# A convolutional LSTM in slots of a whole picture: each gate in two PSUM banks drained by one activation, gates in the order of need, waits counted per gate

## The reference

```python
def _s2s(hprev, w, b, wshift):
    hw = wshift(hprev)
    hd = _shift_down_h(hw)
    return jnp.einsum('bchw,oc->bohw', hd, w[:, :, 0]) + jnp.einsum('bchw,oc->bohw', hw, w[:, :, 1]) + b[None, :, None, None]
...
hmap = jnp.einsum('bchw,oc->bohw', x, w_i2s)
...
def step(carry, _):
    lc, lh, rc, rh = carry
    pre = jax.nn.sigmoid(_s2s(lh, w_left, b_left, _shift_right_w) + left_h)
    o, fg, ig, g = jnp.split(pre, 4, axis=1)
    lc = fg * lc + ig * g
    lh = o * jnp.tanh(lc)
    ...            # the same for rc, rh with the right weights
    return ((lc, lh, rc, rh), None)
(lc, lh, rc, rh), _ = jax.lax.scan(step, (zeros, zeros, zeros, zeros), None, length=h_)
rh = _shift_down_h(rh)
out_h = lh + rh
skip = jnp.einsum('bchw,oc->bohw', out_h, w_skip) + b_skip[None, :, None, None]
return x + skip
```

## Time and profile before

| | |
|---|---|
| median of 3 runs | 6539.12 us (6538.78 to 6540.97) |
| the profiled execution: own time, and span of its trace | 6541.35 us, 6539.6 us |
| busy in the span: PE, PEld, DVE, ACT, POOL | 94%, 56%, 93%, 69%, 39% |
| the untouched layers, from 1863 us on | 4677 us |
| the touched layer | 0 to 1863 us |
| in it the two loops over steps | about 14 to 899 and 935 to 1823 us |

### The profile page before, as it was taken

One profiled execution on the slowest core, in us unless ns is written; L12 is line 12 of the kernel. 1 busy time (PEld: TensorE's weight loads), 2 busy tenths in 40 slices (PEclk: granted clock), 3 DMA queues, 4 the chain that ended last, 5 costly groups with the idle time before them and its releaser, 6 DMA issues. The chain is left out here.

```text
span 6539.6 us, 155482 instructions
## 1 busy us (share of the span) xinstructions
PE 6169.2 (94%) x52289; PEld 3694.8 (56%) x52289; DVE 6112.0 (93%) x3734; ACT 4495.5 (69%) x9597; POOL 2554.8 (39%) x7010
## 2 busy tenths in 40 slices
PE   9999989999969999999999999999999999999996
PEld 2222226556536666666666666666666666666654
DVE  8888878888859999999999999999999999999995
ACT  7888868888836666666666666666666666666662
POOL 4555545555533333333333333333333333333321
PEclk9999999999979999999999999999999999999997
DMA  6666676666642121222212122121222212122114
GB/s 152 156 154 154 155 156 154 153 156 154 154 106 51 41 64 42 59 49 48 56 41 68 44 53 56 41 63 43 59 48 48 56 40 69 44 53 54 41 32 127
DMA packets 904175, 538.20 MB, mean 82 GB/s; under 512 B 695565, under 2 KB 813997, under 8 KB 903597
## 3 DMA queue, kind: packets, MB, share of 16 engines
q1 hardware_dynamic: 903597, 531.10, 34.8%
HBM read 142.32 MB, written 107.35 MB: 38 GB/s over the span
## 5 line engine op out<-in xcount | busy, mean ns | idle before, releaser
L1288 DVE TENSOR_TENSOR_SCAN states<-decay,enter_ps 128x1024 f32<-128x1024 f32 x2048 | 4471.9, 2262 | 55.2 <-PE enter_ps L848 42.4
L1039 ACT ACTIVATE decay<-rate_ps 128x512 f32<-128x512 f32 (+1 forms) x4096 | 2221.6, 594 | 342.9 <-PE rate_ps L834 147.6
L848 PEld LDWEIGHTS enter_ps<-s_steps,s_tokens 128*128 128x128 bf16 x16384 | 1602.8, 129 | 1358.2 <-DVE states L1288 1062.8
L848 PE MATMUL enter_ps<-s_steps,s_tokens 128*128 128x128 bf16 x16384 | 2142.0, 310 | 237.8 <-DVE states L1288 228.0
L834 PE MATMUL rate_ps<-s_wide,s_decays 128*128 128x256 bf16 x8192 | 1318.4, 283 | 8.7 <-DMA s_wide<-rates_dram 8.4
L266 POOL TENSOR_TENSOR entered<-gates 128x512 f32<-128x512 f32 x512 | 901.1, 1760 | 890.2 <-ACT gates L229 890.2
L1211 POOL TENSOR_TENSOR product<-decay,states 128x16 f32<-128x16 f32 x1920 | 465.5, 242 | 1789.2 <-ACT decay L1039 1785.6
L1046 ACT COPY enter_ps<-at_first 128x16 f32<-128x16 f32 x1920 | 337.5, 176 | 1189.1 <-PE enter_ps L848 1134.2
L878 PE MATMUL y_ps<-states,spread 128*32 128x512 f32 x8192 | 1090.3, 604 | 2.4 <-issue 2.4
L834 PEld LDWEIGHTS rate_ps<-s_wide,s_decays 128*128 128x128 bf16 x8192 | 903.1, 118 | 67.5 <-issue 9.9
L186 PE MATMUL pre<-rows,weights_left 128*32 128x512 f32 x8192 | 903.1, 595 | 26.7 <-DMA skip_b<-b_skip 13.7
(11 more groups left out here) (160 smaller groups left out, 2364.4 us busy)
## 6 DMA issues: line engine op xcount, KB each, us to landing
rows<-feat SPq DMA_DIRECT2D x1024, 132.0 KB, 2.4
rows<-feat SPq DMA_DIRECT2D x512, 128.0 KB, 2.4
s_steps<-steps_dram SPq DMA_DIRECT2D x4096, 8.0 KB
rows<-feat SPq DMA_DIRECT2D x512, 127.8 KB, 2.4
s_wide<-rates_dram SPq DMA_DIRECT2D x1024, 32.0 KB, 1.9
s_tokens<-tokens_dram SPq DMA_DIRECT2D x2048, 16.0 KB, 2.0
rates_dram<-parts SPq DMA_DIRECT2D x64, 384.0 KB, 3.3
steps_dram<-parts SPq DMA_DIRECT2D x64, 384.0 KB, 3.5
```

Of the source, the lines that this page charges most:

```text
L848: mm = pe.matmul(out.rearrange("p h l -> p l h"), tokens[s][:, k, :], steps[s][:, k, :, d:d + half], start=True, stop=True)
L1039: act.activation(decay[i][:, half, at:], rate_ps[h][:, :, at:], ACT.Exp).then_inc(decay_ready, 1)
L1288: dve.tensor_tensor_scan(out, factor, term, 0.0, ALU.mult, ALU.add).then_inc(scanned, 1)
```

## The change

A slot becomes one stream's whole picture: 4 slots a step, 256 in all. A gate takes two PSUM banks (`pre[g]`), which eight matmuls fill (a *fill*) and one sigmoid of 128x1024 drains. The fills come in the order input, candidate, forget, output (`FILLS`), and `pre_ready` and `gates_ready` count fills, so that POOL starts after two gates, `forget` after three, and PE refills a gate's banks as soon as that gate of the slot before is drained. ACT puts the tanh of slot k behind the first gate of slot k+1 and ahead of the three others. DVE does `new_features` of slot k ahead of `forget` of slot k+1. All operations of ACT, DVE and POOL work on 1024 elements in a partition, half as many of them. `gates` has two buffers instead of four, of twice the size.

```diff
-GATE_RING = 4
+GATE_RING = 2
+FILLS = (2, 3, 1, 0)
...
-        pre = [ctx.enter_context(nc.psum_tensor(f"pre{c}", [128, 4, BANK], F32)) for c in range(CHUNKS)]
+        pre = [ctx.enter_context(nc.psum_tensor(f"pre{g}", [128, CHUNKS, BANK], F32)) for g in range(4)]
...
-                        for c in range(CHUNKS):
-                            k = s * CHUNKS + c
-
-                            pe.wait_ge(gates_ready, START + (r * STEPS + t) * SLOTS + k - CHUNKS + 1)
-                            for g in range(4):
+                        for i, g in enumerate(FILLS):
+                            pe.wait_ge(gates_ready, START + ((r * STEPS + t) * SLOTS + s - 1) * 4 + i + 1)
+                            for c in range(CHUNKS):
                                 for q in range(GROUP):
-                                    mm = pe.matmul(pre[c][32 * q:32 * q + 32, g, :],
+                                    mm = pe.matmul(pre[g][32 * q:32 * q + 32, c, :],
...
+            def gate_value(r, t, k, i):
+                g = FILLS[i]
+                act.wait_ge(pre_ready, fill(r, t, k, i))
+                if i == 0:
+                    act.wait_ge(feat_ready, slot(r, t, k - GATE_RING))
+                act.activation(gates[k % GATE_RING][:, g, :], pre[g][:, :, :].rearrange("p c l -> p (c l)"), ACT.Sigmoid,
+                               bias=biases[side(k)][:, g:g + 1]).then_inc(gates_ready, 1)
...
                     if following:
-                        gate_values(r, t + (k + 1) // SLOTS, (k + 1) % SLOTS)
+                        gate_value(r, t + (k + 1) // SLOTS, (k + 1) % SLOTS, 0)
                     squash(r, t, k)
+                    if following:
+                        for i in range(1, 4):
+                            gate_value(r, t + (k + 1) // SLOTS, (k + 1) % SLOTS, i)
...
-                        pool.wait_ge(gates_ready, slot(r, t, k))
+                        pool.wait_ge(gates_ready, fill(r, t, k, 1))
...
-                    dve.wait_ge(gates_ready, slot(r, t, k))
+                    dve.wait_ge(gates_ready, fill(r, t, k, 2))
...
                     after = t + (k + 1) // SLOTS, (k + 1) % SLOTS
+                    new_features(t, k)
                     if following:
                         forget(*after)
-                    new_features(t, k)
-                    if following:
                         enter(*after)
```

More of the change, by code:

```diff
@@ L72, in conv_phase @@
         cell = [sb(f"cell{s}", [128, LEN]) for s in range(STREAMS)]
[L73 to L76, removed]
+        gates = [sb(f"gates{i}", [128, 4, LEN]) for i in range(GATE_RING)]
+        forgot = [sb(f"forgot{i}", [128, LEN]) for i in range(2)]
+        entered = [sb(f"entered{i}", [128, LEN]) for i in range(2)]
+        squashed = [sb(f"squashed{i}", [128, LEN]) for i in range(2)]
         weights = [sb("weights_left", [128, 128]), sb("weights_right", [128, 128])]
@@ L209, in slot, with fill @@
             return START + (r * STEPS + t) * SLOTS + k + 1
+        def fill(r, t, k, i):
+            return START + ((r * STEPS + t) * SLOTS + k) * 4 + i + 1
         def steps(eng, r, first, body):
@@ L222, in _ @@
             act.wait_ge(weights_in, START + 7 * DMA)
[L224 to L231, removed]
+            def gate_value(r, t, k, i):
[5 more added lines that the diff above has]
+                               bias=biases[side(k)][:, g:g + 1]).then_inc(gates_ready, 1)
             def squash(r, t, k):
-                c, s = k % CHUNKS, k // CHUNKS
                 act.wait_ge(cell_ready, slot(r, t, k))
-                act.activation(squashed[c][:, :], cell[s][:, BANK * c:BANK * c + BANK],
-                               ACT.Tanh).then_inc(squashed_ready, 1)
+                act.activation(squashed[k % 2][:, :], cell[k][:, :], ACT.Tanh).then_inc(squashed_ready, 1)
             with act.Fori(0, ROUNDS) as r:
@@ L261, in _ @@
                     for k in range(SLOTS):
-                        c = k % CHUNKS
-                        pool.wait_ge(gates_ready, slot(r, t, k))
-                        pool.wait_ge(cell_ready, slot(r, t, k - CHUNKS))
-                        pool.tensor_tensor(entered[c][:, :], gates[k % GATE_RING][:, 2, :],
+                        pool.wait_ge(gates_ready, fill(r, t, k, 1))
+                        pool.wait_ge(cell_ready, slot(r, t, k - 2))
+                        pool.tensor_tensor(entered[k % 2][:, :], gates[k % GATE_RING][:, 2, :],
                                            gates[k % GATE_RING][:, 3, :], ALU.mult).then_inc(entered_ready, 1)
@@ L301, in forget @@
                 def forget(t, k):
-                    c, s = k % CHUNKS, k // CHUNKS
-                    dve.wait_ge(gates_ready, slot(r, t, k))
-                    dve.tensor_tensor(forgot[c][:, :], gates[k % GATE_RING][:, 1, :],
-                                      cell[s][:, BANK * c:BANK * c + BANK], ALU.mult).then_inc(forgot_ready, 1)
+                    dve.wait_ge(gates_ready, fill(r, t, k, 2))
+                    dve.tensor_tensor(forgot[k % 2][:, :], gates[k % GATE_RING][:, 1, :], cell[k][:, :], ALU.mult
+                                      ).then_inc(forgot_ready, 1)
                 def enter(t, k):
-                    c, s = k % CHUNKS, k // CHUNKS
                     dve.wait_ge(entered_ready, slot(r, t, k))
                     dve.wait_ge(forgot_ready, slot(r, t, k))
-                    dve.tensor_tensor(cell[s][:, BANK * c:BANK * c + BANK], forgot[c][:, :], entered[c][:, :],
-                                      ALU.add).then_inc(cell_ready, 1)
+                    dve.tensor_tensor(cell[k][:, :], forgot[k % 2][:, :], entered[k % 2][:, :], ALU.add
+                                      ).then_inc(cell_ready, 1)
                 def new_features(t, k):
-                    c, s = k % CHUNKS, k // CHUNKS
                     dve.wait_ge(squashed_ready, slot(r, t, k))
-                    dve.wait_ge(rows_in[s], START + (r * STEPS + t) * MOVES * DMA)
-                    dve.tensor_tensor(image(feat[s][:, :], CIMG * c), gates[k % GATE_RING][:, 0, :].rearrange(
-                        "p (h w) -> p h w", w=SIDE), squashed[c][:, :].rearrange("p (h w) -> p h w", w=SIDE),
+                    dve.wait_ge(rows_in[k], START + (r * STEPS + t) * MOVES * DMA)
+                    dve.tensor_tensor(whole(feat[k]), gates[k % GATE_RING][:, 0, :].rearrange(
+                        "p (h w) -> p h w", w=SIDE), squashed[k % 2][:, :].rearrange("p (h w) -> p h w", w=SIDE),
                         ALU.mult).then_inc(feat_ready, 1)
```

13 lines of the change are left out of this document (9 added, 4 removed).

## The result

The changed kernel takes 6577.91 us (median of 4 runs, 6574.12 to 6581.84) against 6539.97 for the kernel before: 1.0058 times as long, 95% interval 1.0046 to 1.0070. It is slower by 38 us. That is inside the range of the prediction (6533 to 6587), but its likeliest case, no change at 6539, was wrong, and the rival with a longer ring came true.

What follows compares the result with a forecast made beforehand. PE was taken to bound the loop at 6.90 us a slot, tied by a 6.91 ring. Two rounds, 2 x (1.3 - 2.6) = -2.6 us on 6541.35, gave 6538.7, forecast as 6539 us; range 6533 to 6587.

Steps and rivals of the forecast that it cites:

- ring: Loop: chain from one tanh's end to the next through `feat`, POOL's `entered`, `forgot`, `cell` and tanh; 6.91 us, between 6.80 and 7.29.
- PE's floor: Loop: PE's unchanged count of matmuls needs 2 x 3.45 = 6.90 us for each new slot.
- Sizes: Operations of 1024: `feat`, `forgot`, `cell` 1.23 us each, tanh 1.06, POOL 2.22 once it has its turn, `forgot` behind POOL 1.08.
- The order: DVE does `feat`, then the next slot's `forgot` and `cell`; no DVE work covers a tanh, giving 6.91 us against PE's 6.90.
- POOL's part: POOL's `entered` is asked for during `feat`, gets its turn at `feat`'s end and takes 2.22 us, bounded by 2.11 and 2.28.
- threshold of 6.97: Slot length in the loop from which the kernel would show as slower by over 13 us.
- What late work costs: A ring over 6.90 us delays each of a round's 128 slots; at 6.91 the lag is 1.3 us a round.
- Ends of the rounds: PE's 8.39 us idle after each round's loop shrinks with finer gates, by 2.6 us a round.
- the first gain: Round's end: with the ring early, stream 2's last `feat` ends at 897.0, 3.2 us sooner than 900.24.
- The ring is longer than it looks, and decides: Rival: DVE's `feat`, `forgot`, `cell` with POOL's turn between set the pace; at 7.05 us a slot, 6575 us; chance 0.37.
- the tie: Likeliest case: a ring of 6.87 to 6.97 us equals PE's 6.90; no change, 6539 us; chance 0.42.
- a ring of 5.90: Loop if DVE and POOL shared memory instead of taking turns: `forgot` hidden, 5.90 us, far under PE's 6.90.

Runs made afterwards that it cites:

- DVE's product: The changed kernel with the product `entered` made by DVE between `feat` and `forgot` instead of by POOL: 6535.6 us, 0.9993 of the kernel before.
- the candidate gate first: The changed kernel with the candidate gate's sigmoid also ahead of the tanh, two sigmoids ahead and two behind: 6541.48 us, 1.0004 of the kernel before.
- `forgot` first: The changed kernel with DVE's order of before, `forgot` of the next slot ahead of `feat`: 6818.79 us, 1.0426 of the kernel before.

## Why the prediction was wrong, point by point

**The bound before, and PE's floor.** Right. Every kernel whose ring is short comes to 6.90 us a slot, and the doubled waits of PE cost nothing (full PE with DVE's product).

**Sizes.** Right. `feat` takes 1.226 us, the tanh 1.058, `forgot` ends 1.08 behind POOL. POOL's product of 1024 alone takes 2.37 where 1.27 + 1.08 = 2.35 was worked out.

**The order, "Sum 6.91 us, against 6.90 of PE. The two tie."** This is the step that failed. The mechanism was right and two of its terms were too small; measured, they make the ring 7.04.

The first is POOL's part, 3.48 us from the tanh's end, as if POOL were always held by `feat`. It started 1.16 after the tanh's end (601.10 less 599.94), 0.15 behind its gate, was not held, and ended at 3.54. The prediction had this path as well: a start at 1.12 + 0.08 and the work of 1.27 + 1.08 give its 3.55. It set that aside for the case that POOL "is not ready", but POOL can't end sooner than its start and its own work allow, so the longer of the two paths counts. Its own rows thus gave a ring of 6.98, already over its threshold of 6.97.

The second is `forgot` to `cell`, taken as a hand-over of 0.03, the time between two engines. DVE waiting for its own result needs 0.10 (604.56 to 604.66). 6.91 + 0.06 + 0.07 = 7.04.

A third term was missing: 0.15 once a step in the first slot, so 7.07 on average. All of these are hand-overs. POOL's late start in a step's first slot could be seen before, as the 0.24 of the earlier trace rows, which the prediction used for its range alone; the two on DVE were hidden in the old loop, where other work stood between.

**What late work costs.** Right. 32 steps of 28.29 instead of 4 x 6.895 = 27.58 us are 22.7 more a round; less the 3.2 at its end that is 19.5, and 19.0 and 18.3 were measured. The threshold of 6.97 for a slower kernel was passed by 0.10.

**Ends of the rounds.** Right where the ring is short: with DVE's product PE's wait falls by 3.2 us, the first gain forecast. In the changed kernel that gain is inside the 19.5 above, and PE's own wait does not fall (8.86), since the ring is late by then.

**The rivals and chances.** "The ring is longer than it looks, and decides" named the place, and its example of 7.05 gave 6575. That example was picked and not worked out, so that it came within 3 us is in part luck. The rival had 0.37 against 0.42 for the tie. The text itself said that "five hand-overs add up, and mean latencies only lengthen a ring", and then took each hand-over at the shortest row. With a sum equal to the floor and every hand-over at its shortest, the slower case was the likelier.

**Turns at memory.** The rule quoted from the Trainium skill ("SBUF — State Buffer", section "SBUF: two separate sides") held: in the changed kernel, with the candidate gate first and with `forgot` first, the held operation ends 1.08, 1.07 and 1.07 us behind POOL, and a ring of 5.90, the one without turns, would have left PE full in the changed kernel, which it was not. The turn costs only where both want it: POOL's record in the changed kernel begins 0.10 before `feat`'s ends (601.10 and 601.20) and at 2.38 is no longer than alone.

## What to carry to other kernels

When an engine's order is changed so that it waits for an operation that it has just fed, add up the ring from that operation's end to its next end, and compare it with the bound, not with the busy share: DVE was busy for only 72% of the loop when its ring set the pace. Where two paths lead to the same point, take the longer. If the ring ties with the bound, lean to slower: here each hand-over that the sum forgot made it longer. And where two engines take turns at memory, the slower one's work may be cheaper on the other (1.2 us on DVE for 2.4 on POOL), or earlier, beside something that needs neither.

## What the runs showed of the hardware that was not expected

- DVE waiting for its own last result starts 0.10 us after its end (`cell` behind `forgot`, 604.56 to 604.66), while an operation that doesn't depend on the last one starts 0.08 before its end (with `forgot` first, `cell` behind `feat`, 608.43 to 608.35).
- With the two waits swapped, so that no instruction that makes a wait's value stands between the late wait and the work, the work starts 0.08 us sooner on POOL (0.15 in a step's first slot; 13.5 us less over 256 slots, since `feat` hides a part) and 0.11 sooner on DVE. With none in between, DVE's two waits cost 0.07 more if the late one is written second.
- POOL's product of 1024 fp32 pairs takes 2.37 us and of 512 1.27, 2.15 ns an element; DVE's 1.226 and 0.69, about half of it.
